# Adding the causal bias of the row-maximum scores on VectorE instead of TensorE, in the first layer of a two-layer transformer kernel

## The reference, cut to what matters

```python
def _attention(x, Wqkv, Wproj, bproj):                 # first layer
    ...
    scores = jnp.einsum('bhqd,bhkd->bhqk', q, k) * scale
    causal = jnp.tril(jnp.ones((t, t), bool))
    scores = jnp.where(causal, scores, -jnp.inf)
    attn = jax.nn.softmax(scores, axis=-1)
    out = jnp.einsum('bhqk,bhkd->bhqd', attn, v)
    ...
xm = layernorm(x) * (1 + sc_a) + sh_a                  # modulation by the condition
x = x + gt_a * _attention(xm, ...)
x = x + gt_m * (gelu(xm2 @ W1 + b1) @ W2 + b2)
```

## Time and profile before

| | |
|---|---|
| median of 3 runs | 1240.45 us (1238.41 to 1245.59) |
| profiled execution, its own time | 1243.25 us |
| its span, first to last instruction | 1241.5 us |
| TensorE busy | 1108.3 us, 89% |
| VectorE busy | 805.9 us, 65% |
| ScalarE busy | 624.7 us, 50% |
| GpSimd busy | 245.1 us, 20% |
| mean granted TensorE clock | 0.959 of full speed |

### The profile page before, as it was taken

The page is one execution under the profiler, slowest core; times in us unless marked ns, Lnnn a source line. Parts: engine busy times, 40 slices in busy tenths (PEclk is TensorE's granted clock), DMA queues, the critical chain, the costliest instruction groups (busy, mean ns, idle before and its releaser), DMA issues.

```text
span 1241.5 us, 24238 instructions
## 1 busy us (share of the span) xinstructions
PE 1108.3 (89%) x9228; PEld 967.8 (78%) x9228; DVE 805.9 (65%) x1757; ACT 624.7 (50%) x1255; POOL 245.1 (20%) x250
## 2 busy tenths in 40 slices
PE   3849999899899879999996699999999986999998
PEld 2748888788788657799886588787888764898897
DVE  6536666667666646765763678887888755656653
ACT  1216556556555464342442467777677666433431
POOL 2101111211211124323332111111111103112111
PEclk9769999999999999999998799999999989999999
DMA  5894485356446101000018636465555500001001
GB/s 176 129 257 69 63 156 77 59 79 87 61 70 89 18 9 52 9 10 14 13 36 163 92 54 96 64 90 69 84 75 79 80 3 1 18 18 35 18 18 34
DMA packets 49723, 81.50 MB, mean 66 GB/s; under 512 B 8772, under 2 KB 23332, under 8 KB 48452
## 3 DMA queue, kind: packets, MB, share of 16 engines
q1 hardware_dynamic: 49608, 79.95, 37.2%
HBM read 22.64 MB, written 8.44 MB: 25 GB/s over the span
## 4 chain that ended last, share of the span: by engine, by line
PE 64%; DMA 11%; SPq 9%; DVE 7%; issue 5%; ACT 2%; POOL 1%; POOLq 0%; ACTq 0%; DVEq 0%
PE st_bank L530 13%; PE g_bank L530 10%; SPq L398 9%; PE o_bank L530 7%; PE s_bank L530 6%; PE o_bank L618 6%; DMA k_stack<-qk_split 6%; PE s_bank L579 3%; DMA k_stack<-mask_dram 3%; PE s_bank L585 2%; PE st_bank L598 2%; PE st_bank L600 2%; PE st_bank L604 2%; PE s_bank L581 2%; DVE negmax L1131 2%
## 5 line engine op out<-in xcount | busy, mean ns | idle before, releaser
L796 ACT ACTIVATE probs<-st_bank 128x384 f32<-128x384 f32 (+1 forms) x512 | 276.1, 546 | 165.6 <-PE st_bank L600 94.3
L530 PE MATMUL st_bank<-qk_split,q_stack 128*128 128x512 f32 x768 | 188.7, 404 | 15.6 <-ACT probs L890 11.0
L890 ACT ACTIVATE probs<-st_bank,cols 128x512 f32<-128x512 f32 x128 | 88.0, 689 | 219.4 <-PE st_bank L530 192.9
L1077 DVE TENSOR_REDUCE maxima<-s_bank 128x2 f32<-128x512 f32 x256 | 167.5, 682 | 39.5 <-PE s_bank L585 39.4
L530 PEld LDWEIGHTS st_bank<-qk_split,q_stack 128*128 128x128 f32 x768 | 145.6, 192 | 53.8 <-ACT probs L890 14.4
L1073 DVE TENSOR_REDUCE maxima<-s_bank 128x3 f32<-128x384 f32 x256 | 135.6, 550 | 65.7 <-PE s_bank L581 62.6
L585 PE MATMUL s_bank<-k_stack,q_stack 97*128 97x256 f32 x512 | 118.2, 314 | 27.7 <-DMA k_stack<-qk_split 13.5
L530 PE MATMUL g_bank<-xmT,wa 128*128 128x256 f32 x768 | 128.0, 308 | 8.6 <-POOL xmT L1258 4.7
L618 PE MATMUL o_bank<-probs,v_sb 128*32 128x256 f32 (+1 forms) x2048 | 128.4, 370 | 1.6 <-ACT probs L796 1.6
L585 PEld LDWEIGHTS s_bank<-k_stack,q_stack 97*128 97x128 f32 x512 | 80.2, 196 | 56.4 <-issue 43.5
L530 PEld LDWEIGHTS g_bank<-xmT,wa 128*128 128x128 f32 x768 | 109.9, 208 | 10.0 <-issue 5.6
(11 more groups left out here) (114 smaller groups left out, 2186.6 us busy)
## 6 DMA issues: line engine op xcount, KB each, us to landing
q_stack<-qk_split SPq DMA_DIRECT2D x192, 128.0 KB, 4.5
k_stack<-qk_split SPq DMA_DIRECT2D x192, 128.0 KB, 6.3
gate_rows<-gate_dram SPq DMA_DIRECT2D x32, 128.0 KB, 3.0
wm_f32r<-w_dram SPq DMA_DIRECT2D x4, 1024.0 KB, 10.6
out<-x_sb SPq DMA_DIRECT2D x8, 512.0 KB, 2.9
x_sb<-x_in SPq DMA_DIRECT2D x1, 2048.0 KB, 13.6
q_stack<-q_stack SPq DMA_DIRECT2D x4, 384.0 KB
o_sb<-wa_in SPq DMA_DIRECT2D x1, 1024.0 KB, 6.8
```

The source lines that it names most:

```text
L530: last = mm(dst, weights[i], rows[j], start=(f == 0 and n == 0), stop=(f == tiles - 1 and n == len(TERMS) - 1))
L796: activation(probs[:, h % 8, 0:n], st_bank[h % 2][:, 0:n], ACT.Exp, scale=SCALE)\
L890: activation(h_full[:, m % 2], st_bank[m % 2][:, :], ACT.Gelu, bias=cols[:, cb + m:cb + m + 1])\
L1077: v.reduce_max(maxima[:, gb.mod(2), s, 0:2], bank[:].rearrange("p (i n) -> p i n", n=T), AX.X).then_inc(max_done, 1)
```

## The change

`scores` of the first layer loses its bias matmul. VectorE takes the maximum with two `tensor_tensor_reduce` instructions instead of one `reduce_max`: each adds the bias (float32, from SBUF) to the scores (from PSUM), writes the sum back to the same PSUM columns, and gives the maximum of its block row. The first has 128 columns (query tile 0), the second 256 (query tile 1). The maximum of query tile 1 now comes out whole, so the join of two maxima and its wait go. The wait for `s_ready` is put apart. A buffer `tri_wide` (zeros in columns 0-127, the triangle in 128-255) is new; GpSimd clears its left half at the start, and the triangle's DMA goes there.

```diff
+LOWEST = -3.0e38
...
+        tri_wide = sb("tri_wide", [P, T])
...
-        tri = in_probs(P)
+        tri = tri_wide[:, P:T]
...
-        max_joined = sem("max_joined")
...
                     mm(bank[:, P:3 * P], q[:, P:T], k, start=True, stop=False)
-                    mm(bank[:, 0:P], q[:, 0:P], k[:, 0:P], start=False, stop=False)
-                    last = mm(diagonal(bank), ident16[:], tri16[:].unsqueeze(1).to_broadcast((P, 2, P)),
-                              start=False, stop=True)
+                    last = mm(bank[:, 0:P], q[:, 0:P], k[:, 0:P], start=False, stop=True)
...
-                        dve.wait_ge(s_ready, gb.count(H, s + 1))
+                        if layer == 0:
+                            wait_apart(dve, s_ready, gb.count(H, s + 1), dve_passed)
+                        else:
+                            dve.wait_ge(s_ready, gb.count(H, s + 1))
                         bank = s_bank[S_BANK[s]]
                         if layer == 0:
-                            v.reduce_max(maxima[:, gb.mod(2), s, 0:3],
-                                         bank[:, 0:3 * P].rearrange("p (i n) -> p i n", n=P), AX.X)\
-                                .then_inc(max_done, 1)
+                            for i in range(NT):
+                                keys = slice(i * P, (2 * i + 1) * P)
+                                last = v.tensor_tensor_reduce(
+                                    out=bank[:, keys], in0=bank[:, keys], in1=tri_wide[:, T - (i + 1) * P:T],
+                                    scale=1.0, scalar=LOWEST, op0=ALU.add, op1=ALU.max,
+                                    accum_out=maxima[:, gb.mod(2), s, i:i + 1])
+                            last.then_inc(max_done, 1)
...
-                    if layer == 0:
-                        v.tensor_tensor(m[:, :, 1], m[:, :, 1], m[:, :, 2], ALU.max).then_inc(max_joined, 1)
-                        dve.wait_ge(max_joined, gb.count(1, 1))
...
             set_up_first()
+            dve.wait_ge(power_set, 2)
...
+            g_.memset(tri_wide[:, 0:P], 0.0).then_inc(power_set, 1)
+            g_.memset(half_power[:], -0.5).then_inc(power_set, 1)
             g_.memset(q_stack[:, 0].bitcast(fp32), 0.0).then_inc(stack_set[0], 1)
-            g_.memset(half_power[:], -0.5).then_inc(power_set, 1)
-            pool.wait_ge(power_set, 1)
+            pool.wait_ge(power_set, 2)
```

## The result

The changed kernel takes 1204.58 us (median of 4 runs, 1201.33 to 1205.79) against 1243.02 us before in the same comparison: ratio 0.969, interval 0.9661 to 0.972. It is 38 us faster, where 24.5 were forecast, and its time lies under the range of 1209 to 1262.

What follows compares the result with a forecast made beforehand. TensorE's work plus one stall at each step's end was taken as the bound. Bias matmul 1.54 us and join 0.21 us gave 1.75 a step, 24.5 us over 14 steps, so 1216 us; range 1209 to 1262.

Steps and rivals of the forecast that it cites:

- The join goes too: At the step's end, removing VectorE's join of two maxima shortens the chain by 0.21 us a step.
- the 2.75 us of negation and split: VectorE's negating and splitting of the maxima, from 242.21 to 244.96, counted as 2.75 us of its work in a step.
- I take those as they are: Some first-layer steps take 1.5 us more, one at granted clock 0.93; the prediction left them unchanged.
- TensorE's term: Dropping the bias matmul saves TensorE 0.11 us a head (bounds 0.06 and 0.13), 1.54 us a step.
- only 14 heads count: Savings in slots 0 and 1 only lengthen TensorE's stall at the step's end, so 14 heads count.
- should still wait only for negmax: Sign to look for: after the change TensorE waits only for the negated maxima; other waits would mean VectorE sets the pace.
- VectorE's term: VectorE keeps up: a step without its other waits is 10.07 + 14 C, 20.6 us against TensorE's 21.66.
- C: VectorE's distance from one head's maximum to the next instruction under backlog: 0.465 us before, 0.75 forecast, 0.53 lower bound.
- 0.71 or more: C if a separate instruction reads the maximum, as the Trainium skill says; without it 0.53 us.
- Its limit: VectorE sets the step from C = 0.83; at C = 0.95 the step is 23.4 us, as before.
- The slow rivals: VectorE's instructions don't overlap, C = 1.05, 1259 us, chance 0.15; or elements pass at half rate, 1279 us, chance 0.07.
- half rate: Rival: shared ports halve VectorE's element rate in the new maximum, C = 1.15, 39 us more, 1279 us; chance 0.07.

Runs made afterwards that it cites:

- experiment 2: Kernel before, with the join of two maxima and its wait left out, bias matmul and old reduce kept: 1219.91 us against 1244.6.
- experiment 1: Changed kernel with a small operation on the maxima and its wait put back where the join stood: 1225.63 us, ratio to before 0.9865.
- experiment 6: Changed kernel with a head's 384 columns taken in six VectorE instructions (1252.84 us) or in four (1203.12 us) instead of two.
- experiment 3: Changed kernel with the scores' bias matmul put back beside VectorE's bias, so the bias is added twice: 1217.55 us, ratio to before 0.9807.
- six pieces: Changed kernel with a head's 384 columns taken in six VectorE instructions of 64 columns instead of two: 1252.84 us, ratio to before 1.0082.
- four pieces: Changed kernel with a head's 384 columns taken in four VectorE instructions (64, 128, 64, 128) instead of two: 1203.12 us, ratio to before 0.9696.

## Why the prediction was wrong

**The step that failed** is "The join goes too: from 242.00 to 242.21 on that chain, 0.21 us". That term was mis-sized by a mechanism that I had not looked for. I took the 2.75 us of negation and split as VectorE's own work and moved them up by 0.21. They held 0.65 us of work and two holds by GpSimd. Measured, the join is 1.34 us a step (23.41 to 22.07, experiment 2; 1.33 in experiment 1): 0.2 its own, 1.1 the hold that it set off. Over 14 steps that is 19 us where 3 were counted. Its size hangs on 0.05 us between two starts, which no term of the sum looked at.

Two hints were in the trace of before. The first join of the earlier trace rows takes 0.60 us where the others take 0.17: a GpSimd operation on SBUF runs from 98.86 to 100.14, the join from 99.58 to 100.18, and the negation behind it takes 0.26. And in the second layer, which has no join and where GpSimd starts after the negation, the same line takes 0.25 us:

```profile
758.66 0.25 DVE L1131 TENSOR_SCALAR negmax<-maxima 128x16 fp32r<-128x16 f32 x2
758.94 1.43 DVE L1138 SCALAR_TENSOR_TENSOR negmax<-maxima,negmax 128x8 fp32r<-128x8 f32 x4
```

Two instructions on 16 elements that take 1.35 us, where small ones take 0.18, should have made me ask for the shortest duration of that line. The Trainium skill has the rule (SBUF — State Buffer, "Who interferes with whom": a Vector operation in a two-port mode or with two SBUF inputs shares ports with GpSimd, and whoever issues first has them for the whole instruction). The runs here agree with it: 0.05 us behind GpSimd's start costs 1.1, 0.17 ahead of it costs nothing. The split's operations have two SBUF inputs; the negation has one, and that it runs in a two-port mode is not shown by itself.

**"I take those as they are"**, the four long steps, was the second miss. All four have a granted clock of 0.93, like the one in the earlier trace rows, and the usual ones 1.00; each cost 1.5 us. In the changed kernel the clock is 1.00 from 97.34 to 389.76 us and they are gone: 6 us. They are gone in experiments 1 and 2 too. A single wait of TensorE is shorter on average in all three than the 1.8 us of a usual step before, but experiment 6, where none is over 1.4 us, has four such steps again. What lowers the clock stays open.

**TensorE's term** had the right mechanism and was sized 0.11 us a head; it is 0.08 (0.13 of the bias matmul less 0.05 at the weight load's place), within the bounds of 0.06 and 0.13. In steps, 1.07 us instead of 1.54 (experiment 3). That is near 14 x 0.08 = 1.1, but it doesn't show that only 14 heads count: 16 x 0.08 = 1.3, less what the new wait at the first scores matmul takes back, would give about the same. That wait was missing in the prediction, which said that TensorE "should still wait only for negmax".

**VectorE's term** was right: C is 0.64, between the bound 0.53 and the chosen 0.75. The maximum is read apart, yet C is not "0.71 or more": the reading overlaps the next instruction, so an instruction costs 0.115 us beyond its elements, (0.63 - 0.40) / 2, where 0.065 + 0.09 was counted. Its limit was placed well: six pieces, forecast at 24.0 us a step with the negation corrected, took 24.17 with VectorE never waiting; four pieces cost nothing. The slow rivals were not near: the rows overlap (0.33 us long, 0.25 apart), and 256 elements take 0.47, no half rate.

The sum by usual steps, 14 x (1.34 + 1.07) = 33.7 and 6 for the long ones, is 40 us, 3 more than the 37.0 that the 14 steps gave; they were not all usual, as the first fell only from 21.92 to 21.15. Measured over all 14, the join's part is 23.5 us (329.4 to 305.9, experiment 2, long steps included) and the rest 13.5. The other 5 us between the two spans lie outside these steps, 2.9 of them ahead, and no run explains them. In medians, 24.7 us (experiment 2) and 13 us (experiment 3) make the 38.

## What to carry to other kernels

Before a row's duration goes into a sum, look at the shortest duration of the same line: if it is far below the mean, something holds the instruction, and a change of 0.2 us in its start can be worth five times that. Small VectorE operations on a critical chain are safer ahead of the one that releases a GpSimd operation on SBUF. After a gain, read the waits again before the next step: holding GpSimd back took 1 us out of the chain of each step and the step stayed as long, because the copies of q and k had become the limit. Ask of an instruction order whether the chain's work waits behind work that nobody needs yet: moving the negation ahead of y's bias was worth 34 us of the kernel before, against 11 us for the change once that was done.

## What the runs showed of the hardware

- A two-input operation with a reduced value (bias added in PSUM, maximum kept) passes 384 columns in two instructions at 0.64 us in a row. Start to start, 64 columns take 0.18 us, 128 take 0.25 and 256 take 0.39, so (0.39 - 0.25) / 128 = 1.1 ns a column, against 1.04 in the earlier trace rows. The reading of the maximum (0.14 us long) overlaps the next one.
- GpSimd's operation on SBUF (1.28 us) holds a VectorE operation that starts 0.05 us after it until its end; held back, four operations that took 1.41 us took 0.40.
- Without the bfloat16 matmul between them, the float32 matmul behind a 128-column one shows 0.17 instead of 0.12 us on the chain. That it is the weight load that shows was not tried.
- Twelve transfers of 128 KB a step move at some 130 GB/s, whether SyncE issues all of them or GpSimd two.
